# Edge pass of a graph-attention kernel: four score buffers for two, weighting 11 and scatter 14 groups behind the sums for 10 and 12

## The reference, cut to what matters

```
def _L0_gnn_ref(x, edge_index, edge_attr, W_l, b_l, W_r, b_r, att, bias):
    x_l = (x @ W_l + b_l).reshape(n, H, C)          # H, C = 8, 32
    x_r = (x @ W_r + b_r).reshape(n, H, C)
    src, dst = (edge_index[0], edge_index[1])       # 100000 edges, dst sorted
    x_j = x_l[src]
    g = jax.nn.leaky_relu(x_r[dst] + x_j, NEG_SLOPE)
    alpha = jnp.einsum('ehc,hc->eh', g, att)
    alpha = alpha + jnp.log(edge_attr)[:, None]
    amax = jax.ops.segment_max(alpha, dst, num_segments=n)
    ex = jnp.exp(alpha - amax[dst])
    denom = jax.ops.segment_sum(ex, dst, num_segments=n)
    alpha = ex / (denom[dst] + 1e-16)
    out = jax.ops.segment_sum(x_j * alpha[..., None], dst, num_segments=n)
    return out.reshape(n, H * C) + bias

x = x + _L0_gnn_ref(_layernorm(x, axis=-1), edge_index, edge_weight, ...)   # x is 6250 x 256
x = x + _L0_ffn_ref(_layernorm(x, axis=-1)[None], ...)                      # 8 experts of 512, top 2
```

## Time and profile before

| | |
|---|---|
| median of 3 runs | 2173.49 us (2170.18 to 2184.62) |
| the profiled execution | 2179.18 us, span 2177.4 us |
| first and last gather of `edges` start | 236.4 us, 1524.4 us |
| last `add` of `edges` starts | 1575.5 us |
| busy over the span: PE, DVE, ACT, POOL | 1813.9, 1517.3, 1079.7, 1410.2 us |
| gathers of `edges` | 896 |

### The profile page before, as it was taken

The page is one execution under the profiler, slowest core; times in us unless marked ns, Lnnn a source line. Parts: engine busy times, 40 slices in busy tenths (PEclk is TensorE's granted clock), DMA queues, the critical chain, the costliest instruction groups (busy, mean ns, idle before and its releaser), DMA issues. The chain is left out here.

```text
span 2177.4 us, 41065 instructions
## 1 busy us (share of the span) xinstructions
PE 1813.9 (83%) x9699; PEld 1470.2 (68%) x9700; DVE 1517.3 (70%) x2834; ACT 1079.7 (50%) x2788; POOL 1410.2 (65%) x1370
## 2 busy tenths in 40 slices
PE   0089569998999999999999999899668799999960
PEld 0068357776767767777677767676467699999960
DVE  2966468888888888888788877888687543433325
ACT  0011247666766667666666766676552123233320
POOL 0557677777777777777777777777063555555520
PEclk9999799999999999999999999999956899999985
DMA  4267566666666666666666666666091222222219
GB/s 159 36 212 259 164 181 195 199 180 184 192 179 192 183 181 193 182 193 185 192 180 191 191 181 186 180 197 188 14 346 44 66 70 70 70 71 72 69 54 338
DMA packets 207958, 349.38 MB, mean 160 GB/s; under 512 B 46825, under 2 KB 106097, under 8 KB 207617
## 3 DMA queue, kind: packets, MB, share of 16 engines
q0 software_dynamic: 53760, 150.08, 24.8%
q1 hardware_dynamic: 133096, 177.36, 24.7%
q10 hardware_dynamic: 20936, 20.41, 2.7%
HBM read 292.88 MB, written 56.04 MB: 160 GB/s over the span
## 5 line engine op out<-in xcount | busy, mean ns | idle before, releaser
L733 POOL DMA_INDIRECT rows<-left_rows,idx x896 | 1016.3, 1134 | 279.8 <-issue 263.4
L1055 PE MATMUL p_row<-rights,hotT 128*128 128x256 f32 x1792 | 512.3, 368 | 76.3 <-issue 40.8
L1057 PE MATMUL p_row<-rows,ident 128*128 128x256 f32 x1792 | 539.1, 382 | 0.0
L1123 PE MATMUL p_gain<-W,hots 128*128 128x264 f32 x1792 | 496.1, 401 | 51.4 <-DVE W L895 50.3
L958 ACT ACTIVATE L<-p_row 128x512 f32<-128x512 f32 x448 | 266.9, 596 | 382.5 <-PE p_row L1057 374.6
L1055 PEld LDWEIGHTS p_row<-rights,hotT 128*128 128x128 f32 x1792 | 327.1, 192 | 173.5 <-issue 79.2
L1123 PEld LDWEIGHTS p_gain<-W,hots 128*128 128x128 f32 x1792 | 324.7, 191 | 138.2 <-issue 74.0
L805 DVE TENSOR_TENSOR L<-L,attb 128x1024 f32<-128x1024 f32 x224 | 272.2, 1215 | 60.3 <-issue 36.2
L1015 ACT ACTIVATE far<-iota_row,dl 128x128 f32<-128x128 f32 x896 | 304.9, 392 | 0.0
L895 DVE TENSOR_TENSOR W<-rows,weights 128x1024 f32<-128x1024 f32 x224 | 273.9, 1223 | 26.8 <-ACT weights L1008 23.3
L923 DVE TENSOR_TENSOR acc<-acc,p_gain 128x264 f32 x448 | 189.4, 423 | 143.3 <-PE p_gain L1123 124.2
(11 more groups left out here) (250 smaller groups left out, 1825.6 us busy)
## 6 DMA issues: line engine op xcount, KB each, us to landing
rights<-right_rows SPq DMA_DIRECT2D x448, 256.0 KB
rows<-left_rows,idx POOLq DMA_INDIRECT x896
right_rows<-p_parts SPq DMA_DIRECT2D x50, 256.0 KB, 2.0
c_rows<-results SPq DMA_DIRECT2D x12, 1024.0 KB, 13.4
w<-in_L_ffn_W SPq DMA_DIRECT2D x16, 512.0 KB, 6.4
left_rows<-p_y SPq DMA_DIRECT2D x50, 132.0 KB, 1.8
kept_rows<-X ACTq DMA_DIRECT2D x50, 128.0 KB, 1.9
X<-kept_rows SPq DMA_DIRECT2D x7, 896.0 KB, 10.0
```

What stands on the lines that cost most here:

```text
L733: nc.gpsimd.indirect_dma_start(out=rows[:, g.slot(RINGS), n, :], out_offset=None, in_=d["left"][:, :], in_offset=bass.IndirectOffsetOnAxis ...
L1055: nc.tensor.matmul(to, hotT[:, g.slot(2), i, :], rights[:, g.slot(2), n, part * D:(part + 1) * D], start=(part == 0), stop=False)
L1057: last = nc.tensor.matmul(to, s["ident"][:, :], rows[:, g.slot(RINGS), i, 0:D], start=False, stop=True)
L1123: last = nc.tensor.matmul(p_gain[:, n, 0:D + H], hots[:, g.slot(2), i, :], W[:, g.slot(2), i, :, :].rearrange("p h c -> p (h c)"), start=( ...
```

## The change

`L` gets `APART` = 4 slots for 2, and the two waits on `scored` (in `rectify` and in `put_linear`) ask for a group two further back. `WEIGH` goes from 10 to 11 and `SUM` from 12 to 14. `W`, `hots`, `p_gain` and the ring of `rows` keep their sizes. To make room, `key_row`, which is read once at the start, lies in the first partition of `hots`.

```
-WEIGH, SUM = 10, 12
+WEIGH, SUM = 11, 14
+APART = 4
...
-        L = sb("L", [P, 2, G, H, C + 1])
+        L = sb("L", [P, APART, G, H, C + 1])
...
-        key_row = sb("key_row", [1, 2, CHUNKS * BLOCKS])
...
         hots = sb("hots", [P, 2, G, P])
+        key_row = hots[0:1, :, :, :].rearrange("p a n e -> p a (n e)")[:, :, 0:CHUNKS * BLOCKS]
...
                 def scale(g):
                     wait(v, rectified, 2 * g.n + 2)
-                    own = L[:, g.slot(2), :, :, 0:C].rearrange("p n h c -> p n h c")
+                    own = L[:, g.slot(APART), :, :, 0:C].rearrange("p n h c -> p n h c")
...
                 def put_linear(g):
-                    wait(v, scored, g.n - 1)
-                    nc.vector.tensor_tensor(L[:, g.slot(2), :, :, C:C + 1].rearrange("p n h a -> p n (h a)"),
+                    wait(v, scored, g.n - APART + 1)
+                    nc.vector.tensor_tensor(L[:, g.slot(APART), :, :, C:C + 1].rearrange("p n h a -> p n (h a)"),
...
-                                            L[:, g.slot(2), :, :, :].rearrange("p (b u) h c -> p b u h c", b=2),
+                                            L[:, g.slot(APART), :, :, :].rearrange("p (b u) h c -> p b u h c", b=2),
...
                 def rectify(n):
                     def stage(g):
                         wait(act, summed, 2 * g.n + n + 1)
-                        wait(act, scored, g.n - 1)
-                        nc.scalar.activation(L[:, g.slot(2), PAIR * n:PAIR * (n + 1), :, 0:C].rearrange("p n h c -> p (n h) c"),
+                        wait(act, scored, g.n - APART + 1)
+                        nc.scalar.activation(L[:, g.slot(APART), PAIR * n:PAIR * (n + 1), :, 0:C].rearrange("p n h c -> p (n h) c"),
```

## The result

The changed kernel takes 2167.01 us in the median of 20 runs (2159.67 to 2173.45), against 2178.84 us (2168.86 to 2187.39) for the kernel before, measured beside it: ratio 0.9947, 95% interval 0.9932 to 0.9963. So it is 0.5% faster, some 11.5 us; less than the 1% that I had set as the border of "no change", but clearly on the other side of zero than my 2190. The profiled execution took 2166.91 us.

A forecast was written before the change was run, and what follows sets the result against it. POOL's gathers were taken to bound the edge pass. To the profiled 2179.2 us came +18 for longer gathers and -2 for the end, 2195, hence 2190 us for the median, with a range of 2140 to 2225.

The forecast's parts named there:

- The gathers set the pace: Edge pass: POOL's gathers and their gaps fill 798 of 800 us, so the length of a gather counts.
- How a gather is held: POOL's gathers: one asking during weigh or scale stands still until that ends; weigh's remainder u is 0 to 1.22 us.
- Neither is on the gathers' path: 0 us, as long as gathers hold the pace: Weighting one group later: removed waits of weigh for weights (22.3 us) and gain for weigh (38.9 us) bring 0 us.
- In the steps with the closing work, and in the one or two after, I take DVE to be behind PE already, and nothing moves: DVE's steps around a chunk's closing work: the new wait shifts neither weigh nor scale there.
- The new wait moves `weigh` by 0.71 us and costs 18 us: weigh waits for gain(1) in half the steps: +0.09 us a group, +18 us over 208 groups; bounds -87 and +148.
- (a): The short lock: moved weigh catches the third gather, 5.46 us a group; 2127 to 2142 us, up to 2150; chance 0.17.
- "No preference" for the other half, 5.85: Steps where the new wait does not move weigh: old alignment lost, u 0.61, pace 5.85 us a group.
- The end of the pass, -2 us: After the last weights: 11 groups at 2.3 us against 9 at 2.98, so -2 us, between -4 and +5.
- The ring, no wait: Ring of gathered rows: slack falls from 15 to 8.6 us, 4 to 5 at the loop head; no gather waits.
- (d): The removed waits were the bound: 25 to 45 us come back, 2127 to 2147 us; chance 0.07.
- (b): The long lock: held weigh catches the second gather, 6.08 us a group; +36 to +52, 2208 to 2226 us; chance 0.22.
- (c): The new wait does not move DVE, or gathers don't hang on DVE: only the end changes, 2172 us; chance 0.16.

The follow-up runs named there:

- 10/13: The changed kernel with WEIGH 10 and SUM 13 in place of 11 and 14: 0.996 of the kernel before; 0.9904 and 0.9908 on chips with extra stops.
- 11/13: The changed kernel with SUM 13 in place of 14, WEIGH 11: 0.989 of the kernel before; with two score buffers 0.9885, 2151.12 us.
- 12/14: The changed kernel with WEIGH 12 in place of 11, SUM 14, four score buffers: slower than the kernel before, mean gather 1088 ns.
- 11/14: WEIGH 11 and SUM 14 as in the changed kernel, but with two score buffers: 0.9896 of the kernel before, on chips with extra stops.

## Why the prediction was wrong

Point by point, by its own steps:

- **The gathers set the pace**: right. In the changed kernel, in 10/13, 11/13 and with four slots of `W`, POOL's idle time stays within 0.2 us of 279.8, and the time follows the mean gather; 12/14 is the exception that the ring makes, and without the two multiplications, so without the holds, the program takes 4.6% less than before.
- **How a gather is held** (asks 0.12 us after its start, released with 0.83 us to go, by `weigh` and `scale` only): right where `weigh` is well under way; with both as one-input instructions the mean is 954 ns. It fails where the two start together: u goes to 1.06 and not to 1.22. The reading of the earlier trace rows went wrong there too. `weigh`'s longest, 1296 ns, isn't its length "whatever gather is under way": it is the one at 1143.98, met by a gather that begins 0.04 us behind it and isn't held. So the order of start does count, which the prediction took the trace to speak against: a gather that is there first keeps `weigh` for less than 0.1 us, a `weigh` that is there first keeps the gather for up to 1.06.
- **Four score buffers, 0 us**: right (0.9996; 11/13 with two and with four is the same).
- **"Neither is on the gathers' path: 0 us, as long as gathers hold the pace"**: this is the step that failed. It is true that no gather waits for `weights`, for `weigh` or for PE. But I had just found that a gather's length hangs on when `weigh` comes, and then asked of the removed waits only whether somebody waits for them. The wait for `weights` stretched DVE's step 2 from 4.23 to 5.1 us, and that turned into hold: 8.8 us there before, 2.8 after. With four slots of `W`, so without the new wait, the gathers' run is 15.8 us shorter than before (1273.3 against 1289.1): that is what the new distances are worth, where the prediction has 0. How much of it is the wait for `weights`, PE's wait for `weigh` or the place of `rescale` is not taken apart by any run.
- **"In the steps with the closing work, and in the one or two after, I take DVE to be behind PE already, and nothing moves"**: the same mistake from the other side. DVE is behind there, and just for that reason its period is its own work plus its waits, and the gathers lock to it. And something did move: `rescale` left step 3 for step 5, so that step 3 fell from 4.84 to 4.23 us and its hold from 10.8 to 2.9 us, while step 5 holds 10.6 for 9.3. The order of instructions was known beforehand; no term of the sum has it.
- **The new wait moves `weigh` by 0.71 us and costs 18 us**: mechanism right, sum wrong. `weigh` moved by 0.6, steps 6 and 7 mostly caught the second gather, with 5.82 and 5.94 us a group where I had 6.08 for the long lock, but steps 12 to 15 are near the short one, as rival (a) had it, and with four slots of `W`, without the wait, the gathers take the same time. It nets to about 0. "No preference" for the other half, 5.85, was a guess, and it carried more than half of the 18.
- **The end of the pass, -2 us**: +1.3. I took 2.3 us a group for `weigh`; it comes every 2.88 (2.98 before):

```profile
1555.01 1.23 DVE L896 TENSOR_TENSOR W<-rows,weights 128x1024 f32<-128x1024 f32 x1 [0.65 <-PE p_gain L1124]
...
1557.89 1.22 DVE L896 TENSOR_TENSOR W<-rows,weights 128x1024 f32<-128x1024 f32 x1 [0.65 <-PE p_gain L1124]
```

  Its new wait for `gain(1)` is late next there, 0.65 us each time; I had named it for the steady part and forgotten it here. Without it, with four slots of `W`, the end is 6.4 us shorter.
- **The ring, no wait**: right for 11. The least slack is 3.1 us where I gave 4 to 5, and with one group less 12/14 has none.
- **Rivals**: (d), the removed waits, named part of the cause, with the wrong mechanism and two to four times the size; (a) holds roughly in steps 12 to 15, (b) in part in 6 and 7; (c)'s 2172 is the nearest number and its reason is wrong, since the gathers did change. Of my signs the mean gather, 1117, fell between (c)'s 1134 and (a)'s 1095.

What stays open: why 11/13 settles into its pattern of eight, where PE's sums start 3 to 6 us behind the last gather and not 2 to 3 as in the changed kernel, and gains 24 us; the rule for a single step gives the holds once the periods are known, but not the periods. Also what each removed wait and the place of `rescale` are worth by themselves (a run that moves `rescale` alone would tell), and how much of 11/14's 1% on the chips with extra stops comes from which wait.

## What to carry to other kernels

An engine that never waits can still be slowed by another one: if its instructions are stretched by those of a neighbour, ask of every wait that is added or removed not "who waits for it" but "what does it do to the neighbour's period", and work that out for the steps behind the rare, heavy work as well as for the steady ones. A distance also moves the rare work to another step, and the step that loses it changes its period as if a wait had gone. Distances in a software pipeline have two limits which show in different rows: too short, and the consumer's wait stretches its period; too long, and the ring of buffers runs dry behind the loop head. Here 11/13 lies between them, and the scatter a group further back bought only a wait for the slot of `W`.

## What I had not expected of the hardware

- On some chips the whole program took 2485 us in place of 2177, the kernel before too. The eight traces from there have many extra stops of single engines (POOL 97 to 134 gaps of over 1 us before its gathers, where the kernel before has none elsewhere) and ACT released by `remote`; ratios of schedule changes came out differently there (11/13: 0.9993 against 0.989).
- Useless DVE instructions ahead of `weigh` made the pass no longer, and held the gathers of steps 2 and 3 more (19.1 us) when they were short than when they were long (5.6 us).
- `weigh` and a gather hold each other, but by very different amounts. A gather that starts over 0.045 us behind a `weigh` goes from 0.95 to up to 2.02 us. If the two start within some 0.04 us, it is mostly `weigh` that grows, from 1.22 to 1.30 us at most, and ends 1.25 us after the gather's start, while the gather takes 0.95.
